# Dealing the stages of a 48-loop attention program in a new order

## The reference

```python
# 16 heads of 16; ctx is a second input of the same shape as x
# layer 0: self attention (causal, window of 64, with a slope per head), cross attention, FFN with gelu
x = ln(x + mha(x, x, window_mask, slopes) @ wo + bo)      # attention 0
x = ln(x + mha(x, ctx) @ wo + bo)                         # attention 1
x = ln(x + gelu(x @ w1 + b1) @ w2 + b2)                   # FFN 0, 256 -> 1024 -> 256
# layer 1: the same with a causal mask, every projection a product of two matrices
x = ln(x + mha(x, x, causal))                             # attention 2
x = ln(x + mha(x, ctx)); x = ln(x + gelu_ffn(x))          # attention 3, FFN 1
# layer 2: norms ahead of the attention
x = x + mha(ln(x), ln(ctx)); x = x + silu_ffn(x)          # attention 4, FFN 2
# layer 3
x = ln(x + mha(x, ctx))                                   # attention 5
```

## Time and profile before

| | us |
|---|---|
| median of 3 runs | 3558.05 (3555.76 to 3560.11) |
| the profiled execution: span | 3565.0 |
| PE busy | 3446.8 (97%) |
| DVE busy | 2572.8 (72%) |
| ACT busy | 1935.0 (54%) |
| POOL busy | 1143.4 (32%) |
| mean granted TensorE clock | 0.992 of 2.4 GHz |
| share of DMA queue q1 in the 16 engines' time | 24.0% |

### The profile page before, as it was taken

One profiled execution on the slowest core, in us unless ns is written; L12 is line 12 of the kernel. 1 busy time (PEld: TensorE's weight loads), 2 busy tenths in 40 slices (PEclk: granted clock), 3 DMA queues, 4 the chain that ended last, 5 costly groups with the idle time before them and its releaser, 6 DMA issues.

```text
span 3565.0 us, 53384 instructions
## 1 busy us (share of the span) xinstructions
PE 3446.8 (97%) x18672; PEld 1657.1 (46%) x18932; DVE 2572.8 (72%) x6523; ACT 1935.0 (54%) x2375; POOL 1143.4 (32%) x1049
## 2 busy tenths in 40 slices
PE   8899999999999999999999999999999999999998
PEld 5545544433454554443354455444335445445333
DVE  5766887756886588766778668777577956976667
ACT  2454565555555456555555545555564654655555
POOL 4322432222532242222253223222235322322222
PEclk9999999999999999999999999999999999999999
DMA  6311321223321231122332122112133312211211
GB/s 213 123 46 55 118 67 54 86 60 93 103 78 43 81 114 46 54 87 60 93 123 74 47 93 82 47 53 87 60 109 110 96 54 81 66 46 63 75 54 55
DMA packets 284317, 280.64 MB, mean 79 GB/s; under 512 B 49858, under 2 KB 275266, under 8 KB 280066
## 3 DMA queue, kind: packets, MB, share of 16 engines
q1 hardware_dynamic: 258324, 274.84, 24.0%
q10 hardware_dynamic: 25728, 2.36, 0.6%
HBM read 195.84 MB, written 81.26 MB: 78 GB/s over the span
## 4 chain that ended last, share of the span: by engine, by line
PE 83%; DVE 11%; issue 2%; ACT 2%; DMA 1%; SPq 1%; POOL 0%; another core or an unknown queue 0%; ACTq 0%; DVEq 0%
PE pv L718 14%; PE st L693 14%; PE mx L670 13%; PE mx L768 10%; PE mx L645 10%; PE st L731 9%; DVE row_max L911 5%; PE mx L742 4%; PE st L654 4%; PE mx L765 2%; PE st L778 2%; DVE mx L914 2%; ACT probs L829 1%; DVE turned L934 1%; DMA rows_of_max_dram<-max_rows 1%
## 5 line engine op out<-in xcount | busy, mean ns | idle before, releaser
L829 ACT ACTIVATE probs<-st 128x1024 f32<-128x1024 f32 (+1 forms) x1344 | 1266.6, 977 | 696.4 <-PE st L693 419.1
L911 DVE TENSOR_REDUCE row_max<-mx 128x1 bf16<-128x512 f32 x2048 | 1283.8, 684 | 216.3 <-PE mx L670 121.0
L1021 POOL TENSOR_TENSOR qm<-q_high,own_rows 128x512 bf16<-128x512 bf16 x768 | 797.3, 1044 | 1583.5 <-PE mx L670 1183.6
L670 PE MATMUL mx<-k_high,qm 128*128 128x512 bf16 (+4 forms) x2812 | 815.2, 342 | 44.7 <-DVE row_max L911 18.2
L693 PE MATMUL st<-q_packed,k_packed 97*128 97x512 bf16 (+2 forms) x3072 | 816.0, 346 | 27.3 <-DMA q_packed<-q_parts_dram 9.9
L718 PE MATMUL pv<-probs,va 128*32 128x512 f32 (+2 forms) x6144 | 701.8, 532 | 12.0 <-ACT probs L829 7.1
L670 PEld LDWEIGHTS mx<-k_high,qm 128*128 128x128 bf16 x3072 | 284.3, 98 | 604.0 <-DVE row_max L911 211.1
L914 DVE CUSTOM_DVE_ANT_0 mx<-mx,tab 128x192 f32<-128x192 f32 (+4 forms) x1024 | 400.9, 444 | 132.4 <-PE mx L670 118.7
L693 PEld LDWEIGHTS st<-q_packed,k_packed 97*128 97x128 bf16 (+1 forms) x3072 | 279.6, 98 | 435.0 <-ACT probs L829 149.8
L731 PE MATMUL st<-xT,w1s 128*128 128x512 f32 x768 | 342.9, 592 | 0.0
L957 DVE TENSOR_TENSOR y<-mx,row 128x256 f32<-128x256 f32 x224 | 94.8, 423 | 299.9 <-PE mx L768 297.2
(11 more groups left out here) (88 smaller groups left out, 3141.5 us busy)
## 6 DMA issues: line engine op xcount, KB each, us to landing
k_packed<-k_parts_dram SPq DMA_DIRECT2D x576, 128.0 KB, 2.7
q_packed<-q_parts_dram SPq DMA_DIRECT2D x576, 128.0 KB, 2.7
q_parts_dram<-q_low SPq DMA_DIRECT2D x96, 256.0 KB, 2.2
k_parts_dram<-k_low SPq DMA_DIRECT2D x96, 256.0 KB, 2.5
q_parts_dram<-q_high SPq DMA_DIRECT2D x48, 256.0 KB, 2.1
k_parts_dram<-k_high SPq DMA_DIRECT2D x48, 256.0 KB, 2.3
w1s<-w_dram SPq DMA_DIRECT2D x12, 1024.0 KB, 5.1
w2s<-w_dram SPq DMA_DIRECT2D x12, 1024.0 KB, 7.6
```

The costliest lines, as they stand in the source:

```text
L670: mm = pe.matmul(bank[:, 0:k1 - k0], qm[:, h % RING, i * P:(i + 1) * P], high["k"][s][:, t, k0:k1], start=True, stop=True)
L829: act.activation(dst[:, :, 0:w], held["scores", b, a, n, e][:, :, 0:w], ACT.Exp, scale=ATT_SCALE[a]) \
L911: ins = dve.tensor_reduce(top, scores, AX_X, ALU.max, negate=True)
L1021: pool.tensor_tensor(qm[:, h % RING], high["q"][s][:, h // HT], own_rows[:, h % HT:h % HT + 1].to_broadcast([P, TOK]), ALU.mult) \
```

## The change

All fourteen strings of `MERGE` are replaced. Each new string has as many of each digit as the old one, so the stages of every loop stay, and only their places in the sequence move. Two of the fourteen:

```diff
-    "01": "011110111011101112301210111130111011101121122121011212103111011022111011211110011120010222222222"
-           "0002222020000222002002202220220200202220002222222",
+    "01": "111110101123221102321112110111110211110002110110111021021111101211110110201001110211120220222102"
+           "2202202200220122322022202002222020222022000222000",
...
-    "00": "111230001211101101121110111111011122121011011110010111110101221030011200111002011101101113333023"
-           "33333303033330333333333330003030033330030333300330",
+    "00": "110110111111101110112321211101110111011110121311221101010131011101101110013011332331332333030333"
+           "30303330310020003203303300330333303030300333030032",
```

More of the change, by code:

```diff
@@ L251 @@
 MERGE = {
-    "first": "244014414110101114111101101441111011011101141411101100114141011110110114110001410101112122222222"
-           "2220020224424244422424444422040422220040400220024024222042202422004022000",
-    "01": "011110111011101112301210111130111011101121122121011212103111011022111011211110011120010222222222"
-           "0002222020000222002002202220220200202220002222222",
-    "10": "012301230101210122222113112111020101101110112111010111010110010111011010111002100101101011010001"
-           "10010012222220222002022202222020200202220200002222200220222200220",
@@ L258 @@
[L258 to L277, removed]
@@ L278 @@
-    "00": "111230001211101101121110111111011122121011011110010111110101221030011200111002011101101113333023"
-           "33333303033330333333333330003030033330030333300330",
-    "last": "011101110101101011101011011110101110101110100210100010111212211001010101001001011011011101202001"
-           "000200020000200020000200",
+    "first": "111120441410411011141141101441011141401401411244111011111104401104110444011110100214404101102410"
+           "1421120124222222022424202202010240022224022202202024224200024402202422000",
@@ new lines @@
+    "01": "111110101123221102321112110111110211110002110110111021021111101211110110201001110211120220222102"
+           "2202202200220122322022202002222020222022000222000",
+    "10": "200031100211011110011011112101113102210101101101010110110111102120113202121010121110101122100101"
+           "02222022201202222000120020220200220022022020222002220020202220020",
+    "11": "100110111010002011102111102110112212022011101220010112111012111122211011100121222022001020010022"
+           "1211010100121212220222120202212022202022022202022200022202202200220202002202200",
@@ new lines @@
+    "20": "101100211022211222002211201021111011111211112111211120111101201222211000112200112012000120201011"
+           "002210100210211222122022220212202022220202220002202200022202202222020220",
+    "21": "023201110131210110112112212011111012021101021010110101101011110111012111001121201020101010101212"
+           "220121202022022322220202020220220200022222020002220220020",
+    "30": "012321011021212120101101111010102211130010121110121010201101102111131110110101000201110110101011"
+           "00222102222202220200120202200020222022000222022202020200022220020",
@@ new lines @@
+    "31": "001110101110021001011211012101121220022112210010213103101332313322233101312011220111210221101102"
+           "122320110222012020200021022011210110222231221132222022202020220220202022020220222020222000202220"
+           "020",
+    "40": "100110112101001010011210112111012011201222011021010102110011233012331130233121213031113220122220"
+           "022120110121202220022201010212232101022221123021220232222002220022020022022020202222000022220220"
+           "2022",
+    "41": "200101301221011121112111112111121110111001012010110113101100012101001110101001120110012101201001"
+           "2220222320221202020002200220002222020022302220202020220002220020",
@@ new lines @@
+    "50": "110201030121210110110111101211111211112211110101101101112121011012002311020110001211002010121022"
+           "021223201223202200022002220002020200202000222022022000202202202000",
+    "51": "011021300121110101100111101113100110101101100112110110110110101001110010130011100101221301300113"
+           "102033313333023303303200333023033303003333000033033330333023230030",
+    "00": "110110111111101110112321211101110111011110121311221101010131011101101110013011332331332333030333"
+           "30303033310020003203303300330333303030300333030032",
@@ L282 @@
+    "last": "101101011101101110101020111010101011011011210101010111211011010101100011001101010100101112012200"
+           "002002000200020000200000",
 }
```

## The result

| | before | after |
|---|---|---|
| median of 15 runs, us | 3558.05 (3553.67 to 3563.51) | 3551.24 (3547.63 to 3555.12) |
| ratio | | 0.998 (0.9973 to 0.9988) |
| profiled execution, span, us | 3565.0 | 3545.8 |
| mean granted clock | 0.992 | 0.997 |

The change makes the kernel 6.8 us faster, 0.2%. The forecast was 38 us. One of the 15 runs of after took 3933.9 us at a granted clock of 0.848; it counts in the median (3550.99 without it), not in the range and the ratio.

The account below looks back on a forecast made before the run. The prediction took PE, busy 97% of the span, as the bound. Its terms, 17.5 + 26 - 3 - 3 = 37.5 us, off the median 3558.05 gave 3520.5, predicted as 3520, range 3482 to 3555.

Parts of the forecast that it names:

- It adds and removes no instruction ... I measure an order by PE's own work: Step pricing each order by PE's work, every stage at the timeline's spacing when nothing is late; no size of its own.
- Term for the starts: Starts of loops "01" and "20": PE's shorter waits at first `scores` and less slow clock win 17.5 us, bounds 8 and 23.
- Term for the banks: PE's waits for the `mx` banks, taken as 100 us, fall by 26%: 26 us won, bounds 3.5 and 60.
- Queues: Stages moved past others in engine queues, with a few `turn` to `hidden` distances shorter: 3 us lost, 0 to 10.
- First loop: SP issues the 4.5 MB ahead of the parts of loop (1,0), delaying PE: 3 us lost, from -5 to 9.
- What I had said would show it: Signs: first `scores` idle under 1.5 us, clock above 0.992, bank waits 230 us or less, loops (1,0), (3,0) 47 to 49.
- my sign that the forecast is wrong: Weight loads' waits for row maxima staying at 283 us, or exponentials becoming PE's longest wait.
- Moved, not removed: Rival, 20%: bank waits leave "01" and "20", return in "30", "31", "10": 3543 us, or 3552 at the starts' lower bound.
- Evener over long stretches: Rival, 16%: DVE's backlog builds over more than ten maxima, so bank waits fall 48%: 3498 us, 3485 with the upper bound.

Follow-up runs that it names:

- clear: The changed kernel with six digits moved, so that six DVE stages leave places where POOL is in a long instruction: 3528.86 us, ratio 0.9915 to the kernel before.
- out_late: The kernel before with one digit moved in string 00, so that the second `out` goes behind `load`: 3559.12 us, ratio 1.0.

## Why the prediction was wrong, by its own steps

**"It adds and removes no instruction ... I measure an order by PE's own work".** This is the step that failed. I took every DVE duration from rows in which nothing disturbed it, as if it went with the instruction wherever it stands. In the trace of before, 18 of 288 `scale` instructions began behind a mask or a middle part; in that of after, 66 did. DVE's held time at the three lines, their means less 407, 425 and 170 ns, rose from 18 to 79 us. Freeing `scale` alone gives 36 us back (3551.24 to 3514.97), more than the 31 that the forecast missed. The old order kept the two engines apart, as the rows of before could have told: 260 of its 288 `scale` instructions ran clear of POOL, at 407 ns, and the four behind a `middle` took 1.84 us. I never asked what these long ones had in common.

**Term for the starts, 17.5 us (8 to 23).** About right. In clear the three loops "00" and the three loops "01" behind them are 15.9 us shorter together than in the kernel before, with no wait left and the clock at 1.00, though not all of that need be the starts; "20" adds between 1 and 6.5. The cause that I gave, PE's own work between `middle` and first `scores`, fits clear, and `out` counts for little, as out_late shows.

**Term for the banks, 26 us (3.5 to 60).** The runs speak for a term that was not too large, but was eaten. PE's idle time for row maxima (L911 and L914) is 19.7 us in the old order and 0.8 in the new one when POOL is cut down in both, but 27.4 and 42.7 when it is not. Of the 65 us of the pair without POOL, the first loop has 13 and the starts, by estimate from waits of 1.57, 1.76 and 2.37 us and the clock behind them, some 10; about 42 are left for this term and for masks that are ready sooner, which no run separates. So the term's own size stays open.

**Queues, 3 us lost.** Not seen at the exponentials: weight loads of `scores` waited 149.8 us for them before and 100.7 after. At `turn` PE's idle time grew from 0.7 to 10.2 us, but that is the held `scale` again: with the transpose in its place it is 1.6. I can't give the term a price.

**First loop, 3 us lost (-5 to 9).** Wrong in sign: 77.1 to 63.0 us, 10 to 14 us gained against the 72.8 to 77.1 that the old string took in the seven traces that have it. I took the order of SP's instructions for their times. SP's timeline after, against the earlier trace rows:

```profile
52.88 1.92 SPq L495 DMA_DIRECT2D sq<-squares_dram  x4
64.90 0.33 SPq L486 DMA_DIRECT2D w1s<-w_dram  x1
65.27 0.43 SPq L488 DMA_DIRECT2D w2s<-w_dram  x1
71.27 2.59 SPq L521 DMA_DIRECT2D q_parts_dram<-q_low  x2
```

The bulk stands directly ahead of the parts, but is issued from 52.88 us on, 31 us earlier than before and 18 ahead of the parts. It was all but out of the way when they came, and ACT's wait of 11.80 us and PE's of 5.61 are gone. Only the last transfer of the bulk was still under way when the parts began: it landed at 72.51 us, 7.2 us after its issue. So this case hardly puts to the test the rule that I cited from the Trainium skill, that a DMA engine takes a ring's descriptors in order.

**What I had said would show it.** Right: the first `scores` (no wait left), the clock (0.997), loops (1,0) and (3,0) (47.5, 47.4). Nearly: loop (2,1), 62.4 instead of 61.3. Wrong: the first loop, 14.1 us shorter and not within 9, and the weight loads' waits for maxima, 213.0 + 86.3 = 299 us instead of at most 230, and that was my sign that the forecast is wrong. It warned rightly, but it is a poor measure: with POOL cut down the sum is 275 in the old order and 265 in the new, and the kernels are 65 us apart. Most of what the weight loads wait does not reach PE. The PE rows of the same waits, 27.4 to 42.7 us in sum, were the ones to watch.

**The rivals.** "Moved, not removed" had the right number (3552 at its lower end), but its mechanism, bank waits in "30", "31" and "10" by a larger backlog, was not what happened. None had an instruction that gets longer by where it stands. (In "Evener over long stretches" the 3485 should be 3486.5 by its own terms, 17.5 + 60 - 6 = 71.5; nothing hangs on it.)

## What to carry to other kernels

When only the order changes, ask first which instructions depend on their neighbours on another engine: take each group whose longest instance is several times its shortest, and look at what runs beside those instances. Then price a new order by what it puts side by side, not only by what it puts one behind the other. And an order that already keeps two engines apart has a value that no busy share and no wait of it shows.

## What the runs showed of the hardware

Counted over all instances of the three lines in the trace of after: a `scale` clear of POOL takes 407 ns, at most 416. One that begins behind the start of a mask takes 936 on average and ends some 0.15 us after the mask; L938 behind a mask ends 0.28 us after it (0.425 clear of POOL), L976 0.02 us after. One that begins 0.10 us or more ahead of POOL's keeps its time (L938 13 of 13 with 425 ns, `scale` 4 of 4), and then it is POOL's that gets longer: where at least 0.15 us of DVE's is left, the mask ends 0.90 us after it and takes 1.05 to 1.16 us instead of 1.04, up to 1.29 in the trace of before. Five `scale` instructions whose records begin only 5 to 13 ns ahead of POOL's, while DVE was still ending the one before, were held all the same (1.19 to 1.43 us). Reductions of maxima, which read PSUM, are not held at all, and neither are statistics and transposes, though these read and write SBUF only, like the three that are.

The Trainium skill (SBUF — State Buffer, SBUF: two separate sides) says that VectorE and GpSimd share one pair of ports as "an **exclusive lock**, not a bandwidth split", held for the whole instruction by whichever starts first, and names VectorE instructions in a 2-port performance mode or with two SBUF inputs. The trace agrees for POOL's tensor_tensor, in both directions. It differs for POOL's tensor_scalar with one tensor: there 70 of the 88 `scale` instructions that began behind the start of a mask ended before it did, by 0.62 us on average. By what was measured, that form slows DVE and doesn't lock it out.
